# One transformer stage pair on one core: in the second projection ScalarE normalises, GpSimd adds the output bias during the second attention, and VectorE's last remainder stands behind later sums

## What is computed

```python
x = x + attn_a(layernorm(x), w_qkv, w_out, q_gain)       # causal, 16 heads of 16
x = x + ffn(layernorm(x), router..., wg, wu, wd, sw...)  # 64 experts, 4 per row, and 2 shared ones
x = x + attn_b(layernorm(x), Wqkv, Wproj, bproj)         # not causal, output bias bproj
x = x + ffn(layernorm(x), router..., wg, wu, wd, sw...)  # the same weights again
```

## Time and profile before

| | |
|---|---|
| median of 3 executions | 1188.19 us (1181.44 to 1192.40) |
| the profiled execution | 1184.33 us, its span 1182.7 us |
| busy share of the span: PE, DVE, ACT, POOL | 77%, 61%, 38%, 41% |
| second projection (555 to 675 us): busy PE, DVE, ACT, POOL | 67.4, 73.0, 38.2, 74.5 of 120 us |
| granted TensorE clock there | 0.73 |
| second attention, middle (697 to 793 us): busy PE | 95.6 of 96 us, granted clock 1.00 |

### The profile page before, as it was taken

How to read it: one execution, slowest core, us unless ns; L and a number is a source line. 1 busy time by engine, 2 the same in 40 slices (tenths; PEclk the granted TensorE clock), 3 DMA queues, 4 the chain that set the end, 5 groups by cost and what they waited for, 6 DMA issues and landing times. The chain is left out here.

```text
span 1182.7 us, 23655 instructions
## 1 busy us (share of the span) xinstructions
PE 914.3 (77%) x7706; PEld 696.8 (59%) x7706; DVE 720.7 (61%) x1899; ACT 449.8 (38%) x957; POOL 489.5 (41%) x550
## 2 busy tenths in 40 slices
PE   3985899996999787896556699997989788899000
PEld 2764577765888576684445445545878676677000
DVE  5766877754888433344666689965698643345333
ACT  1553355562211344453233268881211144455000
POOL 3000422216477522332775342221577732231775
PEclk9997899997999898998677779999899998999555
DMA  6294799939964588973486467802623498985443
GB/s 238 43 172 80 152 187 220 233 130 256 214 184 142 174 259 255 284 234 119 118 202 186 76 94 114 116 7 70 153 99 107 158 265 257 266 260 175 118 131 115
DMA packets 159015, 197.06 MB, mean 167 GB/s; under 512 B 17328, under 2 KB 137648, under 8 KB 155824
## 3 DMA queue, kind: packets, MB, share of 16 engines
q1 hardware_dynamic: 99744, 94.56, 36.7%
q0 software_dynamic: 22848, 68.18, 18.2%
q10 hardware_dynamic: 36304, 32.84, 9.2%
HBM read 132.86 MB, written 90.18 MB: 189 GB/s over the span
## 5 line engine op out<-in xcount | busy, mean ns | idle before, releaser
L856 ACT ACTIVATE tmp<-ps 128x256 f32<-128x256 f32 (+1 forms) x328 | 145.5, 472 | 127.2 <-PE ps L809 37.3
L949 ACT ACTIVATE tmp<-ps 128x384 f32<-128x384 f32 (+1 forms) x256 | 135.6, 543 | 71.5 <-PE ps L622 46.9
L485 POOL DMA_INDIRECT xd<-big,slot x128 | 129.3, 1010 | 61.7 <-issue 37.8
L524 POOL DMA_INDIRECT big<-yd,slot x128 | 126.5, 988 | 42.7 <-issue 25.0
L453 POOL COPY arena<-negmax 24x2048 bf16<-24x2048 bf16 x32 | 60.5, 1892 | 175.8 <-ACT negmax L856 175.8
L603 PE MATMUL ps<-arena 96*128 96x256 bf16 (+1 forms) x512 | 106.2, 279 | 13.1 <-DVEq L290 10.6
L1086 DVE SCALAR_TENSOR_TENSOR X<-big,comb,X 128x256 f32<-128x256 f32 x128 | 59.2, 484 | 77.6 <-DMA big<-yd,slot 77.2
L1473 DVE SCALAR_TENSOR_TENSOR tmp<-tmp,ps 128x128 f32<-128x128 f32 x128 | 36.7, 287 | 113.2 <-ACT tmp L1017 112.5
L619 PE MATMUL ps<-arena 120*128 120x256 bf16 (+1 forms) x512 | 100.9, 265 | 0.9 <-POOL arena L453 0.3
L1483 DVE COPY tmp<-ps 128x256 f32<-128x256 f32 x128 | 53.6, 424 | 66.7 <-PE ps L838 36.4
L809 PE MATMUL ps<-ident,big 128*128 128x128 f32 x512 | 74.3, 290 | 25.0 <-ACT tmp L856 15.0
(11 more groups left out here) (173 smaller groups left out, 1906.5 us busy)
## 6 DMA issues: line engine op xcount, KB each, us to landing
big<-xd POOLq DMA_DIRECT2D x128, 256.0 KB, 4.9
arena<-parts SPq DMA_DIRECT2D x192, 128.0 KB, 6.0
xd<-zero SPq DMA_DIRECT2D x8, 2048.0 KB, 14.2
spill<-in_we SPq DMA_DIRECT2D x128, 128.0 KB
yd<-tmp POOLq DMA_DIRECT2D x64, 256.0 KB, 3.5
yd<-tmp ACTq DMA_DIRECT2D x64, 256.0 KB, 3.5
parts<-arena SPq DMA_DIRECT2D x128, 96.0 KB
arena<-in_we SPq DMA_DIRECT2D x8, 1024.0 KB, 8.9
```

Of the source, the lines that this page charges most:

```text
L485: pool.indirect_dma_start(xd[:, :], bass.IndirectOffsetOnAxis(ap=slot[:, i, k:k + 1], axis=0), xn_all[:, i, :], None).then_inc(scattered.s ...
L524: pool.indirect_dma_start(gring[n % GRING], None, yd[:, :], bass.IndirectOffsetOnAxis(ap=slot[:, b * TB + m % TB, m // TB:m // TB + 1], ax ...
L856: return act.activation(dst, src, ACT.Copy)
L949: act.activation(prob[h % 8][:, 0:n], ps[2 + h % 2][:, 0:n], ACT.Exp).then_inc(exp_ready.sem, 1)
```

## The change

ScalarE makes the normalised rows of the second projection: VectorE computes, beside the reciprocal, the shift minus mean times reciprocal (`bshift`), and ScalarE writes xn = X times brstd plus bshift with two instructions. ScalarE writes the second part of q and k behind the copy of `xt` instead of ahead of it. VectorE's `split_last(b-2)` stands behind the first two sums of batch b instead of at the end of the batch before. The bias addition goes from VectorE to POOL, into the attention, behind the first spread of each batch.

```diff
@@ gpsimd, attention
                     if s < B:
                         spread_maxima(s, 0)
+                    if s < B and r == 1:
+                        xb = X[:, s * TB:s * TB + TB, :]
+                        pool.wait_ge(*neg_spread(r, 2 * s + 1))
+                        pool.tensor_tensor(xb, xb, bproj[:, :].rearrange("p (a d) -> p a d", a=1).broadcast_to([P, TB, D]),
+                                           ALU.add).then_inc(bias_added.sem, 1)
+                        pool.wait_ge(bias_added.sem, s + 1)
@@ scalar, projection
                         act.activation(bsd[:, :], bve[:, :], ACT.Sqrt).then_inc(bsd_ready.sem, 1)
-                    if has[last] and r == 1:
-                        second_part(s - 1, 1 - i)
+                        act.wait_ge(brstd_ready.sem, 2 * (s + 1))
+                        act.wait_ge(*xT_done(r, s))
+                        for tt in range(TB):
+                            act.activation(xn[:, tt, :], X[:, s * TB + tt, :], ACT.Identity, bias=bshift[:, tt:tt + 1],
+                                           scale=brstd[:, tt:tt + 1]).then_inc(xn_ready.sem, 1)
                     if has[0]:
                         act.wait_ge(*xT_done(r, s + 1))
                         act.wait_ge(*v_done(r, s))
                         copy(xt[:, :, :].rearrange("p c n -> p (c n)"), ps[0][:, :]).then_inc(xt_ready.sem, 1)
+                    if has[last] and r == 1:
+                        second_part(s - 1, 1 - i)
@@ vector
-            def batch_normalise(b):
-                dve.wait_ge(*xT_done(1, b))
+            def batch_scale(b):
                 dve.wait_ge(bsd_ready.sem, b + 1)
+                dve.wait_ge(*xn_ready(1, b * TB))
                 dve.reciprocal(brstd[:, :], bsd[:, :]).then_inc(brstd_ready.sem, 1)
-                dve.wait_ge(brstd_ready.sem, b + 1)
+                dve.wait_ge(brstd_ready.sem, 2 * b + 1)
                 settle()
-                for tt in range(TB):
-                    dve.tensor_scalar(xn[:, tt, :], X[:, b * TB + tt, :], bmv[:, tt, 0:1], brstd[:, tt:tt + 1],
-                                      ALU.subtract, ALU.mult).then_inc(xn_ready.sem, 1)
+                dve.scalar_tensor_tensor(out=bshift[:, :], in0=bmv[:, :, 0], scalar=-1.0, in1=brstd[:, :],
+                                         op0=ALU.mult, op1=ALU.mult).then_inc(brstd_ready.sem, 1)
-            def add_bias(b):
-                xb = X[:, b * TB:b * TB + TB, :]
-                dve.wait_ge(*xn_ready(1, (b + 1) * TB))
-                dve.tensor_tensor(xb, xb, bproj..., ALU.add).then_inc(bias_added.sem, 1)
@@ vector, second projection
                     for b in range(B + 1):
                         if b < B:
-                            combine(0, b, b % 2)
+                            combine(0, b, b % 2, range(0, 2))
+                        if b >= 2:
+                            split_last(b - 2)
+                        if b < B:
+                            combine(0, b, b % 2, range(2, TB * K))
                             batch_norm(b)
                         if b >= 1:
                             split_rest(b - 1)
                         if b < B:
-                            batch_normalise(b)
-                            add_bias(b)
-                        if b >= 1:
-                            split_last(b - 1)
+                            batch_scale(b)
+                    split_last(B - 1)
```

More of the change, by code:

```diff
@@ L101, in build @@
         bsd = sb("bsd", [P, TB])
+        bshift = sb("bshift", [P, TB])
         mhalf = sb("mhalf", [P, NT])
@@ L1074, in normalise, with combine @@
                                       ALU.subtract, ALU.mult).then_inc(done.sem, 1)
-            def combine(run, b, i):
-                for m in range(TB * K):
+            def combine(run, b, i, terms=range(TB * K)):
+                for m in terms:
                     k, tt = m // TB, m % TB
@@ L1125, in split_last @@
                 dve.tensor_tensor(pt[b % 2][:, 2, :], res, pt[b % 2][:, 1, :], ALU.subtract).then_inc(p3_ready.sem, 1)
-            def add_bias(b):
-                xb = X[:, b * TB:b * TB + TB, :]
-                dve.wait_ge(*xn_ready(1, (b + 1) * TB))
-                dve.tensor_tensor(xb, xb, bproj[:, :].rearrange("p (a d) -> p a d", a=1).broadcast_to([P, TB, D]),
-                                  ALU.add).then_inc(bias_added.sem, 1)
             for r in range(2):
```

## The result

The changed kernel takes 1196.3 us (median of 20 runs, 1187.44 to 1200.76) against 1187.27 (20 runs) for the kernel before on the same chip: a ratio of 1.0076, 95% interval 1.0053 to 1.0099. That is 9.0 us slower, within the 1% called no change in the prediction; the forecast was 1194 us with a range of 1183 to 1204. The 20 runs of the changed kernel fall in two groups, 8 of them between 1187.44 and 1191.05 and 12 between 1195.94 and 1200.76, with none in between; the profiled one is the lowest of the upper group, and by the means the difference is 8.0 us.

The account below looks back on a forecast made before the run. The second projection was taken as a chain of waits, the second attention's middle as bound by PE. +6.1 us at the last batch's turn, +1.4 at the attention's start and +0 make +7.5 on 1186.4: 1194 us, range 1183 to 1204.

Parts of the forecast that it names:

- The turn: Second projection: T(b), the start of batch b's turn on PE, comes 0.5 us later for every turn.
- The third part and the queue: Second projection: late split_last(1) delays batch 1's stores by 3.3 us, then SP's loads, batch 2's stores, batch 4's first part.
- T(5) moves by 3.3 + 0.5 = +3.8: Second projection: batch 5's turn on PE starts 3.8 us later, 3.3 from SP's queue and 0.5 from the turn.
- The bound of 0 for this term: SP's queue, second projection: shift of 0 instead of 3.3 us if all traffic, not their start, sets the loads' end.
- Rival 4: Second projection: loads' end independent of start, batch 4's gather earlier, no store wait; 1 to 4 us less, about 1184; 0.15.
- The last batch: Second projection's end: POOL's casts hold bve and the shift; T(6) to T(7) 15.75 instead of 13.95 us, +1.8.
- rival 2: Last batch's shift not held by the cast, or attention's start free: 3.2 or 1.4 us less, 1190 to 1192; 0.18.
- The attention's start: Second attention: bias ahead of mark_heads(2) delays POOL's cast and at least VectorE's second small cast, +1.4 us on PE.
- The middle: Second attention's middle: POOL's bias add takes 1.2 us, VectorE's cast waits 0.1 us, swallowed by idle time; cost 0.
- Rival 3: Second attention: POOL's add slow, from about 1.5 us, holding VectorE's casts every batch; +6 us, 1200; 0.20.
- The sum: Whole kernel: +6.1 us at T(7), +1.4 at the attention's start, +0 in its middle: +7.5 us, 1194; 0.47.

Follow-up runs that it names:

- the second pair: before_again and after_again, the kernel before and the changed kernel repeated without edits on a second chip: 1302.14 and 1306.06 us, one execution each.
- a_spread: Changed kernel, SP's loads of stacks 0 and 1 in the second projection spread 4 per batch between stores: 1185.86 us, ratio 0.9975 to before.
- b_spread: Kernel before, SP's 24 loads of stacks 0 and 1 in the second projection spread 4 per batch between stores: 1175.62 us, ratio 0.9897.
- b_norm: Kernel before, only the normalisation moved to ScalarE with VectorE writing the shift; remainders keep their order, bias stays on VectorE: 1192.88 us, ratio 1.005.
- after_again: Changed kernel, unedited, run again on the second chip for a second profile: 1306.06 us, one execution.
- a_marks: Changed kernel, POOL's two casts released by the landing of the last gathers instead of the last sum: 1306.99 us, ratio 1.0048 to before.
- c_b: b_spread, with constant rows of key stacks 0 and 1 written by ScalarE in batches 1 to 4 instead of POOL's casts: 1276.67 us, ratio 0.9963.
- b_bias: Kernel before, only the output bias moved from VectorE to POOL in the second attention: 1302.02 us, ratio 1.0003.
- the first four experiments: b_split, b_norm, b_spread and a_spread, run together on one chip: 1189.68, 1192.88, 1175.62 and 1185.86 us; before took 1187.15 there.
- c_a: a_spread, ScalarE writing the rows instead of POOL's casts, POOL's first bias addition behind its second spread: 1280.32 us, ratio 0.9966 to before.
- b_split: Kernel before, only ScalarE's second part behind the copy of xt and split_last(b-2) behind two sums of batch b: 1189.68 us, ratio 1.0025.
- before_again: Kernel before, unedited, run again on the second chip for a second profile: 1302.14 us, one execution.

## Why the prediction was right, point by point

**The turn: right.** Each ordinary turn was forecast 0.5 us later. The shift takes 0.16 and 0.15 for handing over, `xn` on ScalarE 1.09 (forecast 1.03 from overlap, 1.13 without). PE's wait ahead of a turn grew from 2.27 to 2.82, so +0.55. What the step left out is that PE takes longer over the same matmuls in some batches (last section; whether the change makes these more frequent is not shown): T(2) is +2.0 where three turns give 1.5, and T(3) is +4.0 where four give 2.0.

**The third part and the queue: the mechanism right, its size not in the profile.** `split_last(1)` was forecast to end 3.3 us later, near 599.3. It ended 3.9 later (596.44 + 1.23 = 597.67, entry 2.17 earlier). The loads begin 3.9 us later, as they must, standing behind the stores of batch 1. But "T(5) moves by 3.3 + 0.5 = +3.8" measured +8.4: the stretch of the loads moved 190 GB/s at a share of 1.04, and before, in the like stretch, 221 (second row; the first is for the last section):

```profile
594.17:600.50 6.33, 5.64 (x20) 4.63 (x21) 4.94 (x10) 1.27 (x3) 5.00 (x5) 0.73 0.58 145
...
606.00:626.00 20.00, 13.10 (x37) 10.19 (x38) 11.71 (x26) 4.71 (x8) 15.43 (x16) 0.67 1.02 221
```

The extra 4.6 us did not repeat in the second pair: with `split_last(1)` late by 2.5 us, T(5) came 1.1 us earlier than before. The bound of 0 for this term, "if the end of the loads is set by all traffic and not by when they begin", fits that pair and not the first. By a_spread against b_spread the change costs 0.74% without this term, and 0.76% with it.

**Rival 4: its first half happened.** T(4) came 0.7 us early in spite of four late turns: ahead of it PE waited the ordinary 2.82 us and not the 6.15 of before, so no gather held it this time. In b_norm, where the loads begin 2.6 us later, T(4) came 1.2 us late. Its second half, no wait for a store, came nearly true in after_again (0.95 us) and not in the profiled execution after, where the wait grew to 11.51 us with full DMA engines (share 1.04), the reason given against it.

**The last batch: right.** Forecast: `bve` to the end of the first cast, the shift by the second for over 3 us, the interval T(6) to T(7) at 15.75. Measured: 1.90 for `bve` (over 2 was named as the sign), 3.24 and 15.33. The first half of rival 2, a shift that passes, happened in a_spread, and without its gain: `split_rest` was held in its place. a_marks shows that the hold can be moved, but lands on another batch; in c_b, with the casts off POOL, it is gone.

**The attention's start: right, a little too dear.** +1.4 was forecast, +1.1 measured, in the changed kernel (16.72 to 17.79) and in b_bias (17.81), so the second half of rival 2 is out. One of VectorE's casts slips through, as the step had it, and the second takes 3.46.

**The middle: right.** POOL's addition takes 1.26 to 1.27 us where 1.2 was taken from twice the copy; the next cast of maxima takes 0.18. Rival 3, whose point of decision was 1.5 us, is out. The estimate from the Trainium skill (GPSIMD Engine Reference, "Elementwise — side-by-side cycle accounting") of 1.1 to 1.2 us lies a little under the measured time.

**The sum: right, in part by luck.** Forecast +7.5 from T(7) 6.1 and the start 1.4; the medians have +9.0 (about 6 to 12 by the interval), the profiled pair +11.6. By the ratios of the parts it is: remainders +0.25%, normalisation +0.50%, bias +0.03%, together 0.78% against 0.76% measured (b_bias on another chip, each part uncertain by 0.3% or more). The forecast led the sum through the queue: +3.8 at T(5), where measured it is +8.4 in one pair and -1.1 in the other. That the total holds all the same has a reason in the prediction's own terms: without the block, eight turns of 0.5, 1.8 at the last batch and 1.4 at the attention's start make 7.2 us, nearly the 7.5 with it. a_spread against b_spread has 0.74% (about 5 to 12 us), 10 us by the medians. Their profiles show 4.5 us of it up to the end of the attention. The rest lies behind it, in the expert stage, whose length from `rstd` to the end varies from 359 to 368 us between the profiled executions of before, after and the first four experiments. Whether the change lengthens it is not shown; on the third chip that stage was shorter in c_a (395.7 us) than in c_b (400.5). So the total was right, and where in the kernel the medians lose it is known for about half. One slip stands in the range: rival 3 with its price doubled gives 1206 on the forecast of 1194, not 1204; the result does not touch it.

## What to carry to other kernels

Before work is taken off an engine, read whether that engine's work stands in the chain: here VectorE lost 13 us of busy time and the chain through ScalarE grew by 0.5 us a turn. A block of loads in a queue that also carries the stores of the loop is worth looking at first: spreading 24 loads over six batches gave 1%, more than any arithmetic moved here. A VectorE instruction with two SBUF inputs, however small, can cost the rest of a long POOL cast beside it; to start the cast earlier, or to let the small instruction come later, only chose another victim here.

## What the runs showed of the hardware

**The same matmuls take 5.2 to 6.8 us in a projection.** The 16 matmuls of q and k in batch 2 took 5.21 us before and 6.45 after (PE's timeline of before; the row of after stands under the result):

```profile
595.51 5.21 PE L559 MATMUL ps<-xt,wqk 128*128 128x256 f32 x16 [0.69 <-ACT xt L856]
```

The windows of that stretch have a granted clock of 0.73 of full speed before, and of 0.55, near the lower of the two levels (1.2 GHz), after. PE had stood 2.27 us ahead of the turn in the one case and 2.82 in the other. In batches 0 to 4 after the stretch takes 6.39, 5.38, 6.45, 5.41 and 6.47 us; before 6.00, 5.41, 5.21, 6.74 and 5.37. The longer wait is not needed for a slow stretch: batch 3 of before took 6.74 us behind a wait of 2.27, and b_split, where VectorE still normalises, has slow stretches in batches 2, 4, 5 and 7 (6.71, 6.78, 6.67, 6.67 us). Its batch 2 on PE:

```profile
589.82 0.66 PE L542 MATMUL ps<-ident,xn 128*128 128x128 f32 x4 [2.39 <-DVE xn L1112]
591.16 6.71 PE L559 MATMUL ps<-xt,wqk 128*128 128x256 f32 x16 [0.69 <-ACT xt L856]
```

The granted clock from 589.82 to 597.87 us is 0.58. What makes a stretch slow stays open, so the further microseconds of T(2) and T(3) after are not shown to come of the change.

**ScalarE stood idle with no releaser on the second and third chip.** There before takes 1304.58 and 1290.9 us instead of 1187. ScalarE's waits in before_again (total us, times, longest):

```profile
ACT tmp L988 <- remote: 90.3, 7, 16.5
...
ACT big L856 <- remote: 52.3, 5, 26.8
...
ACT tmp L895 <- remote: 19.6, 1, 19.6
```

These 13 pauses are 162 us, and after_again has 11 such of 164 us; the profiles of before, after and the first four experiments have none. They are more than the 117 us between before's medians on the first and the second chip; that they make the difference was not tested. What ScalarE waits for is not in the trace, and stays open; it is why kernels are compared here on one chip, but for the places where the text names another.
